# Three narrow products per tile in place of one wide product and a reduction, in a graph-attention kernel

## The reference

```python
z  = (h @ W_gat[l]).reshape(n, 4, 32)
el = sum(z * attn_l[l], -1);  er = sum(z * attn_r[l], -1)
e  = leaky_relu(el[src] + er[dst], 0.2)
m  = segment_max(e, dst);  ex = exp(e - m[dst])
alpha = ex / segment_sum(ex, dst)[dst]
h_gat = segment_sum(alpha[:, :, None] * z[src], dst)
```

## Time and profile before

| | us |
|---|---|
| three runs, median | 13884.4 (13879.9 to 13896.82) |
| the profiled execution, its own time | 13875.03 |
| its span, first to last instruction | 13873.3 |
| DVE busy in it | 10723.6 (77%) |
| PE busy, PEld busy | 8685.8 (63%), 7028.6 (51%) |
| POOL busy, ACT busy | 6951.8 (50%), 2809.5 (20%) |

### The profile page before, as it was taken

How to read it: one execution, slowest core, us unless ns; L and a number is a source line. 1 busy time by engine, 2 the same in 40 slices (tenths; PEclk the granted TensorE clock), 3 DMA queues, 4 the chain that set the end, 5 groups by cost and what they waited for, 6 DMA issues and landing times. The chain is left out here.

```text
span 13873.3 us, 209115 instructions
## 1 busy us (share of the span) xinstructions
PE 8685.8 (63%) x52858; PEld 7028.6 (51%) x52859; DVE 10723.6 (77%) x16335; ACT 2809.5 (20%) x4518; POOL 6951.8 (50%) x7719
## 2 busy tenths in 40 slices
PE   4663577767778678773566636773666665666664
PEld 3552255553566446553555524552555554555554
DVE  7666479964899559985888867998677877677777
ACT  0110222223222232220444412221000000000000
POOL 3774057730777227760777706773344443344442
PEclk8555788878788788886888856665788888788887
DMA  4335754437444464451555612222233333333333
GB/s 179 113 112 131 266 165 105 104 53 295 112 105 104 113 260 106 105 93 28 141 147 145 141 23 51 54 54 23 86 96 92 93 95 69 95 93 93 95 93 65
DMA packets 720170, 1523.50 MB, mean 110 GB/s; under 512 B 364796, under 2 KB 416585, under 8 KB 680627
## 3 DMA queue, kind: packets, MB, share of 16 engines
q0 software_dynamic: 306624, 795.04, 24.1%
q1 hardware_dynamic: 413427, 727.07, 15.4%
HBM read 1050.48 MB, written 471.10 MB: 110 GB/s over the span
## 5 line engine op out<-in xcount | busy, mean ns | idle before, releaser
L967 POOL DMA_INDIRECT h<-table,edges_ring x3984 | 3785.5, 950 | 1291.0 <-issue 1161.1
L1146 PE MATMUL bank<-h,edges_onehot 128*128 128x260 f32 (+1 forms) x7968 | 2150.6, 431 | 717.6 <-DVE acc L1307 396.4
L1146 PEld LDWEIGHTS bank<-h,edges_onehot 128*128 128x128 f32 x7968 | 1693.8, 263 | 1130.2 <-DVE acc L1307 458.7
L1241 DVE TENSOR_TENSOR_SCAN bank<-edges_fresh,edges_top,bank 4x1024 f32<-4x1024 bf16 x660 | 1542.0, 2336 | 426.8 <-PE bank L1121 426.8
L967 POOL DMA_INDIRECT edges_rows<-table,edges_ring x1512 | 1492.3, 987 | 465.0 <-issue 415.7
L1121 PE MATMUL bank<-ident,edges_score 128*4 128x128 f32 x5280 | 1017.2, 358 | 953.1 <-DVE edges_score L1271 797.3
L1248 DVE TENSOR_TENSOR_SCAN edges_top<-edges_fresh,bank 4x1024 f32<-4x1024 bf16 x660 | 1497.0, 2268 | 0.2
L956 POOL COPY edges_ring<-src_idx 128x8 uint32 (+1 forms) x440 | 90.7, 207 | 2759.4 <-PE bank L1146 1356.4
L1121 PEld LDWEIGHTS bank<-ident,edges_score 128*4 128x4 f32 x5280 | 495.9, 104 | 1266.9 <-DVE edges_score L1271 841.9
L1307 DVE TENSOR_TENSOR acc<-acc,bank 128x260 f32 (+1 forms) x2640 | 919.8, 348 | 206.1 <-DVE acc L1297 59.8
L2010 POOL DMA_INDIRECT rec<-dst,slots x782 | 797.1, 1019 | 433.6 <-issue 433.2
(11 more groups left out here) (345 smaller groups left out, 16680.7 us busy)
## 6 DMA issues: line engine op xcount, KB each, us to landing
table<-x SPq DMA_DIRECT2D x154, 1040.0 KB, 7.9
edge_score<-edge_feat SPq DMA_DIRECT2D x220, 512.0 KB, 3.7
table<-h SPq DMA_DIRECT2D x77, 1040.0 KB, 7.9
table<-source_typed_rows SPq DMA_DIRECT2D x63, 1040.0 KB, 8.1
h<-table,edges_ring POOLq DMA_INDIRECT x3984
edge_feat<-edge_score SPq DMA_DIRECT2D x110, 512.0 KB, 3.0
dst_row<-dst_rows SPq DMA_DIRECT2D x71, 704.0 KB, 4.2
buf<-rec SPq DMA_DIRECT2D x44, 840.0 KB, 5.2
```

The lines of the kernel that those rows point to most:

```text
L967: pool.indirect_dma_start(out=rows[s % R][:, j, :], out_offset=None, in_=table, in_offset=bass.IndirectOffsetOnAxis(ap=ring[:, s * ST + j: ...
L1146: ins = pe.matmul(sum_b[k % 3], onehot[s][:, j, :], rows[s][:, j, A0:W], start=j == k * GT, stop=j == (k + 1) * GT - 1)
L1241: v.tensor_tensor_scan(score_b[0:HEADS, :], fresh[s][:, 0:SLOTS_SB], score_b[0:HEADS, :], top[1 - s][:, SLOTS_SB - 1:SLOTS_SB], ALU.add, A ...
```

## The change

`spread_dst` makes three products of four columns for each tile, one for each part k, that accumulate in the same four PSUM columns, where it made one of twelve columns. The stationary operand of the three is the same; it is loaded for each. The moving operand of each has its own start address (k bf16 numbers further) and a step of three. DVE's three-part addition (L1276) and its buffer `spread` go, the addition of L1278 reads PSUM directly, and the link count LA falls by one. The convolution passes keep their two links.

```diff
-        arg, spread = p.buffer("arg", (P, ST, HEADS)), p.buffer("spread", (P, ST, HEADS))
+        arg = p.buffer("arg", (P, ST, HEADS))
...
-        narrow_b, dst_b = flip_b[:, 0:512].bitcast(BF16), flip_b[:, 512:512 + 3 * ST * HEADS]
+        narrow_b, dst_b = flip_b[:, 0:512].bitcast(BF16), flip_b[:, 512:512 + ST * HEADS]
...
                     for j in range(ST):
-                        ins = pe.matmul(dst_b[:, j * 3 * HEADS:(j + 1) * 3 * HEADS], flippedT[s][:, j, :],
-                                        dst_parts(g)[:, bass.ds(bins[j // GT], 1), 0:3 * HEADS]
-                                        .rearrange("p b c -> p (b c)"), start=True, stop=True)
+                        parts = dst_parts(g)[:, bass.ds(bins[j // GT], 1), 0:3 * HEADS].rearrange("p b (h k) -> p (b h) k", k=3)
+                        for k in range(3):
+                            ins = pe.matmul(dst_b[:, j * HEADS:(j + 1) * HEADS], flippedT[s][:, j, :], parts[:, :, k],
+                                            start=k == 0, stop=k == 2)
                     ins.then_inc(dst_spread, 1)
...
-                LA = 3 if scored_edges else 2
+                LA = 2 if scored_edges or conv is not None else 1
...
-                    c.link(v.tensor_reduce(spread[:, :, :].rearrange("p t h -> p (t h)"),
-                                           dst_b.rearrange("p (b k) -> p b k", k=3), AX, ALU.add))
-                    c.link(v.tensor_tensor(sc, zrows(s)[:, :, :, DH], spread[:, :, :], ALU.add))
+                    c.link(v.tensor_tensor(sc, zrows(s)[:, :, :, DH], dst_b.rearrange("p (t h) -> p t h", h=HEADS), ALU.add))
```

## The result

On the same chip the changed kernel took 14237.65 us (median of 4 runs, 14228.77 to 14247.4), the kernel before 13886.08 (4 runs, 13879.9 to 13896.82): a ratio of 1.0252, interval 1.0235 to 1.027. It is slower, as forecast, but by 352 us and not by 148, outside the stated range of 13880 to 14135. The profiled execution took 14228.77 us, 353.7 more than that of before.

A forecast was written before the change was run, and what follows sets the result against it. Bound: a 1.44 us DVE, PE, ACT, DVE loop ending each superblock. 3 x 106 x 0.40 = 127 us plus 106 x 0.20 = 21, together 148, gave 14023 profiled, 14032 median; range 13880 to 14135.

The forecast's parts named there:

- The bound: End of an attention superblock: a 1.44 us loop through DVE, PE's turn_top, ACT's rate and DVE's subtraction sets the time.
- Part 1: DVE's three-part addition L1276 goes: value 0, as the subtraction's release does not move; gain at most 66 us.
- part 2: DVE's addition L1278 reads PSUM directly: 0.19 to 0.25 us, not on the loop, so 0.
- Part 3: PE's spread_dst, 24 products in place of 8: 12 address instructions per superblock, not 4; 1.0 us more on the sequencer.
- split of a pair: Sequencer cost of a pair of tiles in spread_dst: 3 x 0.075 + 6 x 0.026 = 0.38 us, 1.50 per superblock.
- What hides it: PE's idle time before turn_top absorbs part of the delay, leaving 0.40 us per superblock in network 0, 0.20 in network 2.
- the lower clock: Case of PE granted the lower clock more often in longer superblocks: 0.6 instead of 0.4 us each, 14096 us.
- The spacing of 0.026 us: L1094 products on PE's array start 0.026 us apart in the record, so 16 more cost 0.42 us.
- A: Rival: the parts share one address instruction in spread_dst; 0 to 0.1 us per superblock, say 13893 us; chance 0.16.
- B: Rival: each product in spread_dst makes its own address instruction; 615 us more, 14500 us; chance 0.08.
- C: Rival: it gets faster, with cheap addresses, the subtraction freed and POOL's gathers bounding at 10.11 us; 13818 us; chance 0.07.

## Why the prediction was right in its mechanism and wrong in its size

**The bound.** Right for the first chip as far as its trace shows: `turn_top`'s place in TensorE's order carried the delay into rate and weights, and DVE's share fell while the time rose. DVE was busy 81 us less (110 forecast).

**Part 1 and part 2 at nothing.** 0.9983 with the reduction left out agrees, on the other chips. On the first it wasn't measured alone.

**Part 3, twelve address instructions, 1.0 us more on the sequencer.** The count is exact (5280), and so is what it makes of the stretch: 1.72 us forecast from the copy to `turn_top`, 1.73 measured. The even 0.124 us between the address instructions show that they pace it; the forecast's split of a pair into 3 x 0.075 and 6 x 0.026 gave nearly the same sum (0.38 us against 3 x 0.124 = 0.37), but the products between them add nothing of their own. What the time would be on that chip without them wasn't tested. On the others they make 0.012 of 0.054, and getting them out of the way gives 0.019.

**What hides it: the step that failed.** It gave 0.40 us a superblock in network 0 and 0.20 in network 2; measured are 1.0 to 1.15 and about 0.1. Behind the copy the step was well sized: the chain there has grown by 0.24 + 0.12 = 0.36 us. What it missed are the 0.71 us ahead of the copy. It took the sums and flips of TensorE as they were, and they got longer, by 0.57 us between the first and the twelfth sum alone. The rows had shown the danger. The superblock of the earlier trace rows had 5.57 us of sums at the lower clock, and its period was 11.37; the next had sums of 2.90 us at the higher one and 10.34. The forecast read the first as rare and its length as a matter of how much idle time was filled (0.5 us in the mean). But before, the slack that was there (0.50 us before `turn_top`) also absorbed moderately slow sums: from 2.5 to 4.5 us of them the period stayed near 10.3. The change used up the slack, so that any slow stretch of TensorE now goes into the period, and it came with a lower clock (0.83 to 0.75). The table by length of the sums says how much: where they took 3.6 to 4.0 us, a superblock got 0.33 us longer, about the 0.40 of the forecast; from 4.0 to 4.5 us 0.69; above, 1.7, and these went from 8 to 34 of 102. The prediction did price the lower clock, at 0.6 in place of 0.4 us, 14096; these 0.2 us are a third of the 0.65 that were missing (1.05 less 0.40). In network 2 `turn_top` starts 2.81 us behind the copy in the mean before and 2.52 after, so the copy was early and the delay was smaller than forecast, inside its bounds.

**The spacing of 0.026 us.** From it the forecast took 0.42 us for sixteen products on the array. The experiments show that the spacing of starts in the record is no price: sixteen products recorded 0.026 us apart lengthen a superblock by 1.6 us on the other chips. On the first chip nothing shows such hidden time: 98% of the flips' signals come within 0.02 us of the recorded end. But no product was added there by itself.

**The rivals.** A and B fall by the count, 5280 and neither 1760 nor 10560. C falls by the time. All three shared the assumption that broke, that the rest of TensorE's work would not get slower.

**What stays open.** It isn't known whether the lower granted clock on the first chip comes from the sixteen products, from the longer superblock, or both; no experiment ran on a chip like it. That the lower clock is what lengthened the sums is read from the windows (0.51 with 5.57 us, 1.00 with 2.90) and from the correlation of -0.99, and not tested by a run. Why a filler costs 3.4% on before and 0.3% on after is open as well. No version that was run and keeps all three parts beats the kernel before: the best is 1.003, the fall product first.

## What to carry to other kernels

Don't give work to an engine because its busy share is low: eight products and a reduction were cheaper than twenty-four products. On the first chip the three addresses per pair are the price that the trace shows, 0.124 us each; on the others the kernel before pays some 0.1 us for a small product whatever its columns. Before pricing a delay by the mean idle time it can fill, look at what else that idle time absorbs, here the swings of TensorE's clock, and price the kernel as if it were gone. And a term that rests on the spacing of TensorE's recorded starts needs a second support, such as when the waiting engine goes on.

## What the runs showed of the hardware that was not expected

The same kernel took 13886 us on one chip and 15984 to 16020 on others, 15% apart, with recorded durations alike: the convolution superblock was 17.08 and 19.8 us long, the attention one 10.3 and 13.0, both 2.7 more. There, waiting engines go on up to 4 us behind TensorE's recorded ends. The Trainium skill, "Perfetto Trace Analysis", section "Tensor Engine Instruction (MATMUL, LD_WEIGHTS)", says that the end in TensorE's record is estimated from the instruction's size and not observed; the 3.04 us from the flips' recorded end to ACT's copy agree.

A register-computed address that differs from another only by a constant is an instruction of its own on TensorE's sequencer here: three for each pair of tiles, 5280 in all, used twice each. In a run of them they start 0.124 us apart on either kind of chip. On the slower chips eight more of them in a superblock lengthen it by 0.45 us, 0.056 each, less than their spacing, so part of it is hidden there.
